# Decoder block on one core: parts of keys and queries stored as they are made, and new orders in the first unit and the handover

## The reference

```python
x_norm = _layernorm(x, norm_g, norm_b)                 # the mamba block, once forward, once on reversed time
xi, z = split(x_norm @ in_w.T);  u = silu(conv(xi) + conv_b)
xdbl = u @ xp_w.T;  dt = softplus(xdbl[..., :16] @ dt_w.T + dt_b);  Bm, Cm = xdbl[..., 16:32], xdbl[..., 32:]
h = exp(dt * A) * h + (dt * u) * Bm;  y = sum(h * Cm)  # a scan over 512 steps, 512 channels x 16 states
y = (y + u * Dp) * silu(z);  x = x + (y_fwd + flip(y_bwd)) @ out_w.T / 2;  x = x + gelu(norm(x) @ w1.T + b1) @ w2.T + b2
scores = q @ k.T / 4, where mask == 0: -1e9            # 16 heads of 16 features, keys and values from the context
out = softmax(scores) @ v @ wo.T + bo
h = relu(norm(x) @ W_fc.T) ** 2;  y = h @ W_proj.T     # then five steps of a threshold unit with reset
```

## Time and profile before

| | |
|---|---|
| time, median of 3 runs | 2777.25 us (2776.8 to 2777.51) |
| profiled execution's own time | 2776.59 us |
| its span (first to last instruction) | 2774.8 us, so 1.8 us lie around it |
| busy in the span | PE 95%, PEld 65%, DVE 79%, ACT 63%, POOL 62% |
| mean granted TensorE clock | 0.98 of full |
| mamba pass, then attention pass | about 1618 us, then 1157 us |

### The profile page before, as it was taken

How to read it: one execution, slowest core, us unless ns; L and a number is a source line. 1 busy time by engine, 2 the same in 40 slices (tenths; PEclk the granted TensorE clock), 3 DMA queues, 4 the chain that set the end, 5 groups by cost and what they waited for, 6 DMA issues and landing times. The chain is left out here.

```text
span 2774.8 us, 55530 instructions
## 1 busy us (share of the span) xinstructions
PE 2633.1 (95%) x19210; PEld 1798.9 (65%) x19210; DVE 2203.8 (79%) x3271; ACT 1743.1 (63%) x2899; POOL 1715.4 (62%) x962
## 2 busy tenths in 40 slices
PE   5999999999999999999999878999999999999996
PEld 2787787787787778877887744455554545454523
DVE  3999999999999899999999959584848484858573
ACT  4778878877877888788778423535354544444342
POOL 1898989988988998899899812323233232323130
PEclk9999999999999999999999989999999999999978
DMA  3122121302221221222122052304040404040300
GB/s 122 33 80 81 63 65 65 103 28 78 88 67 54 79 81 48 79 66 95 36 77 101 9 158 78 99 25 116 8 121 2 121 2 121 2 121 2 106 2 15
DMA packets 102089, 187.07 MB, mean 67 GB/s; under 512 B 14720, under 2 KB 75264, under 8 KB 100256
## 3 DMA queue, kind: packets, MB, share of 16 engines
q1 hardware_dynamic: 101840, 183.92, 21.3%
HBM read 148.38 MB, written 35.52 MB: 66 GB/s over the span
## 5 line engine op out<-in xcount | busy, mean ns | idle before, releaser
L1087 POOL TENSOR_TENSOR hC<-h,C_rep 128x1024 f32<-128x1024 f32 x512 | 1201.3, 2367 | 100.6 <-DVE h L945 94.1
L945 DVE TENSOR_TENSOR_SCAN h<-dA,pair 128x512 f32<-128x512 f32 x1024 | 1171.3, 1201 | 107.8 <-PE pair L467 96.5
L698 ACT ACTIVATE dA<-delta,cols 128x511 f32<-128x511 f32 x1024 | 664.1, 711 | 41.7 <-DVE h L945 28.3
L467 PE MATMUL pair<-diagB,duT 64*128 64x128 f32 x8192 | 549.0, 281 | 23.4 <-DVE h L945 15.2
L467 PEld LDWEIGHTS pair<-diagB,duT 64*128 64x128 f32 x8192 | 486.2, 188 | 124.5 <-issue 92.7
L558 PE MATMUL y_bank<-ident,hC 128*128 128x128 f32 x4112 | 537.3, 277 | 5.5 <-POOL hC L1087 4.5
L558 PEld LDWEIGHTS y_bank<-ident,hC 128*128 128x128 f32 x4112 | 456.3, 141 | 97.7 <-issue 55.7
L1820 DVE CUSTOM_DVE_ANT_0 masked<-pair,mask_bias 128x512 f32<-128x512 f32 x512 | 322.2, 686 | 19.1 <-PE pair L1325 13.5
L1563 ACT ACTIVATE pr<-pair 128x1024 f32<-128x1024 f32 x256 | 248.3, 1021 | 74.3 <-PE pair L1325 74.3
L1922 POOL CAST m_part<-m_rest 8x512 bf16<-8x512 f32 x16 | 9.6, 602 | 429.1 <-ACT m_rest L1563 429.1
L467 PE MATMUL general<-xnT,w_in 128*128 128x512 f32 x512 | 250.5, 605 | 10.9 <-ACT zs L698 5.1
(11 more groups left out here) (177 smaller groups left out, 3166.8 us busy)
## 6 DMA issues: line engine op xcount, KB each, us to landing
C_rep<-c_rows SPq DMA_DIRECT2D x128, 512.0 KB, 4.3
qk_parts<-qk_part SPq DMA_DIRECT2D x96, 256.0 KB, 3.9
w_in<-w_in SPq DMA_DIRECT2D x16, 1024.0 KB, 4.9
k_st<-qk_parts SPq DMA_DIRECT2D x8, 1536.0 KB, 9.1
q_st<-qk_parts SPq DMA_DIRECT2D x8, 1536.0 KB, 9.2
x_in<-x SPq DMA_DIRECT2D x18, 512.0 KB, 5.3
w_out<-w_out SPq DMA_DIRECT2D x17, 512.0 KB, 4.2
mid<-x_out SPq DMA_DIRECT2D x9, 512.0 KB, 4.7
```

Of the source, the lines that this page charges most:

```text
L467: return pe.matmul(o, lhsT, rhs, start=start, stop=stop)
L698: return act.activation(o, i, fn, **kw)
L945: last = dve.tensor_tensor_scan(h[:, g % 4, i, :], dA[:, g % 4, i, :], dBu[:, i, :], 0.0, ALU.mult, ALU.add)
L1087: pool.tensor_tensor(hC[:, g % RING], h[:, g % 4], C_rep[:, 2 * j:2 * j + 2, :], ALU.mult).then_inc(s_hC.sem, 1)
```

## The change

Three places are touched; the arithmetic stays.

1. **Stacks.** The writes of keys and queries to memory go part by part: the three bands of part 0 after `high`, the two of part 1 after `middle`, the one of part 2 after `cut_last`. This holds at the handover and in every iteration.
2. **First unit.** The norms come ahead of `A_log`; z goes to four banks of its own (`first_z`), between the xi blocks; silu of `u` is done by block (`first_u`), `x_proj` follows by block; POOL makes all eight first diagonals, two of them ahead of `make_du`; PE transposes `ab` and spreads the first pair ahead of two of the z blocks of unit 1; ACT makes decays between the z evacuations.
3. **Handover.** The last output projection moves behind `handover` as keys `("lo", jj)`: one half after the key projection, the other after the query projection, which now precede the values. Its add and its store move with it. ACT writes the ones of `k_st`; the row mask work moves behind the query's cuts; sequence 1's `first_norm` no longer waits for the store; POOL's `take_x1(0)` and what follows it wait for the mask tiles, since `mask_i` now lies where `x1` is.

```diff
     (attention_keys)
-    before = many("w2", 2) + many("k", KD) + many("v", 2) + many("qn", KD) + many("q", KD)
+    before = many("w2", 2) + many("k", KD) + [("lo", 0)] + many("qn", KD) + many("q", KD) + [("lo", 1)] + many("v", 2)
     (mamba_pass, PE)
-            for k in range(KI):
+            for k in range(KI - 1):
                 for kk in range(KD):
                     in_proj(("xi", k), 0, 0, k, kk, BEFORE)
-            for k in range(KI):
-                for kk in range(KD):
-                    in_proj(("z", k), 0, 0, k, kk, BEFORE)
+            for k in range(2):
+                first_z(k)
+            for kk in range(KD):
+                in_proj(("xi", KI - 1), 0, 0, KI - 1, kk, BEFORE)
+            for k in range(2, KI):
+                first_z(k)
...
             dt_proj(0, 0, 0, BEFORE)
-            for k in range(KI - 1):
+            for kk in range(KD):
+                in_proj(("xi", KI), 1, 0, 0, kk, BEFORE)
+            for kk in range(KD):
+                in_proj(("z", KI), 1, 0, 0, kk, BEFORE)
+            du_rows(0, 0, 0, BEFORE)
+            pe.wait_ge(kinds["z"][1].sem, kinds["z"][1].count(KI - 1))
+            spread_du(0, 0)
+            for k in range(1, KI - 1):
                 for kk in range(KD):
                     in_proj(("z", KI + k), 1, 0, k, kk, BEFORE)
-            for kk in range(KD):
-                in_proj(("xi", KI), 1, 0, 0, kk, BEFORE)
-            du_rows(0, 0, 0, BEFORE)
-            spread_du(0, 0)
...
-            for jj in range(TT // 2):
-                for half in range(2):
-                    out_proj(jj, half, TT + jj, 2 * B - 1, AFTER)
     (mamba_pass, ACT)
-            act.wait_ge(setup.sem, setup.count(0))
...
+            for k in range(2):
+                first_z(k)
+            first_u(0)
+            start_conv(KI - 1, 0, 0, KI - 1, BEFORE)
+            first_z(2)
+            first_u(1)
+            first_z(3)
+            for k in range(2, KI):
+                first_u(k)
+            act.wait_ge(kinds["z"][1].sem, kinds["z"][1].count(KI - 1))
+            f(zs[0][:, :, :], zs[0][:, :, :], ACT.Silu).then_inc(z_silu.sem, 1)
+            act.preload_act_table_set("natural_log_exp_and_others")
...
-            for j in DIAG_ACT:
-                diagonals(0, j)
-            for k in range(KI - 1):
-                take_z(KI + k, 1, 1, k, BEFORE)
             start_conv(KI, 1, 1, 0, BEFORE)
+            take_z(KI, 1, 1, 0, BEFORE)
             take_du(0, 0, 0, BEFORE)
-            for g in range(3):
-                decay(0, 0, g)
+            act.wait_ge(setup.sem, setup.count(0))
+            decay(0, 0, 0)
+            take_z(KI + 1, 1, 1, 1, BEFORE)
+            decay(0, 0, 1)
+            take_z(KI + 2, 1, 1, 2, BEFORE)
+            decay(0, 0, 2)
     (mamba_pass, POOL)
+            first_diagonals((0, 1))
             make_du(0, 0, 0)
-            for j in DIAG_POOL:
-                diagonals(0, j)
+            first_diagonals(range(2, NP))
     (attention_pass, SP)
-                sp.wait_ge(s_part.sem, s_part.count(2 * beta + n))
-                for band, part in enumerate(which):
-                    dma(s_qkw, qk_dram[n, band].rearrange("(k p) t -> p k t", p=P), qk_part[:, n, part])
+                for part in range(3):
+                    if part < 2:
+                        sp.wait_ge(qk_hi.sem, qk_hi.count(4 * beta + 2 * n + part))
+                    else:
+                        sp.wait_ge(s_part.sem, s_part.count(2 * beta + n))
+                    for band in range(6):
+                        if which[band] == part:
+                            dma(s_qkw, qk_dram[n, band].rearrange("(k p) t -> p k t", p=P), qk_part[:, n, part])
...
-            sp.wait_ge(early.mid.sem, early.mid.count(B))
             x_used(0)
             load_x(1)
...
             stacks(1, 0)
+            sp.wait_ge(kinds["lo"][1].sem, kinds["lo"][1].count(1))
+            dma(early.mid, mid[B * TT:(B + 1) * TT].rearrange("j p f -> p j f"), early.tiles[0][:, :, :])
     (attention_pass, PE)
-            for jj in range(TT // 2):
-                project_v(jj, BEFORE)
+            last_out(0)
+            query_input(0, BEFORE)
             pe.wait_ge(setup_dve.sem, setup_dve.count(0))
...
-            query_input(0, BEFORE)
             project_q(BEFORE)
+            last_out(1)
+            for jj in range(TT // 2):
+                project_v(jj, BEFORE)
     (attention_pass, DVE)
-            dve.memset(k_st[6 * DH:QR, :, :], 1.0)
...
             cut_lo(0, 0)
-            dve.tensor_scalar(keep[:, :, :], maskT_i[:, :, :], 0.0, MASKED, ALU.is_equal, ALU.mult)
+            add_last(0)
...
             cut_last(0, 0)
+            dve.drain()
+            take_q(BEFORE)
+            cut_lo(0, 1)
+            dve.tensor_scalar(keep[:, :, :], maskT_i[:, :, :], 0.0, MASKED, ALU.is_equal, ALU.mult)
+            cut_last(0, 1)
+            add_last(1)
+            first_norm(1)
+            dve.drain()
+            dve.tensor_tensor(mask_biasT[:, :, :], keep[:, :, :],
+                              not_full[:, :].unsqueeze(1).broadcast_to((P, TT, T)), ALU.mult)
             for jj in range(TT // 2):
                 take_v(jj, BEFORE)
...
-            take_q(BEFORE)
-            cut_lo(0, 1)
-            cut_last(0, 1)
-            dve.wait_ge(early.mid.sem, early.mid.count(B))
-            first_norm(1)
     (attention_pass, POOL)
             rstd_of(FF1, 1)
+            pool.wait_ge(setup_dve.sem, setup_dve.count(1))
             take_x1(0)
```

More of the change, by code:

```diff
@@ L71 @@
     gelu: Stage
+@dataclass
+class Late:
+    yT: object
+    w_out: object
+    res: object
 def attention_keys():
@@ L141, in mamba_keys @@
 def mamba_keys():
-    before = [("nf", k) for k in range(KD)] + [("xi", k) for k in range(KI)] + [("z", k) for k in range(KI)]
+    before = [("nf", k) for k in range(KD)] + [("xi", k) for k in range(KI)]
     before += [("xd", 0), ("bt", 0), ("dt", 0)]
-    before += [("z", KI + k) for k in range(KI - 1)] + [("xi", KI), ("tr", 0)]
+    before += [("xi", KI), ("z", KI), ("tr", 0)] + [("z", KI + k) for k in range(1, KI - 1)]
     def batch(units):
@@ L169, in batch @@
         return keys
-    return before, apart(batch(4)), apart(batch(2) + [("yb", 2 * KI)] + [("op", TT + jj) for jj in range(TT // 2)])
+    return before, apart(batch(4)), apart(batch(2) + [("yb", 2 * KI)])
 BEFORE, AFTER = "before", "after"
@@ L500, in x_proj @@
                     pe.wait_ge(s_wxp.sem, s_wxp.count(X))
+                if isinstance(b, str) and b == BEFORE:
+                    pe.wait_ge(first_silu.sem, first_silu.count(kk))
+                elif kk == 0:
                     pe.wait_ge(u_silu.sem, u_silu.count(X))
@@ L815, in _, with first_z, first_u @@
             last.then_inc(a_log.sem, 1)
-            act.wait_ge(setup.sem, setup.count(0))
+            def first_z(k):
+                act.wait_ge(*G.full(("z", k), BEFORE))
+                f(zs[0][:, k, :], bank[k][:, :]).then_inc(G.done_sem(("z", k)), 1)
+            def first_u(k):
+                act.wait_ge(s_tap.sem, s_tap.count((CW - 1) * k + CW - 2))
+                f(u[0][:, k, :], u[0][:, k, :], ACT.Silu).then_inc(first_silu.sem, 1)
             for norm in norm_steps(0):
@@ L988, in add_out @@
                                   ALU.add).then_inc(G.done_sem(("op", i)), 1)
+            first, second = norm_steps(0)
+            for fn in first:
+                fn()
             dve.wait_ge(a_log.sem, a_log.count(0))
@@ L994, in _ @@
             last.then_inc(setup.sem, 1)
-            first, second = norm_steps(0)
-            for fn in first:
-                fn()
             dve.memset(hC[:, :, :, :], 0.0)
@@ L1122, in _, with attention_pass @@
             pool.sem_inc(handover.sem, 1)
-def attention_pass(nc, ctx, a, mid, out, sb, where, stage, psum, consts, handover, early):
+    return Late(yT, w_out, res)
+def attention_pass(nc, ctx, a, mid, out, sb, where, stage, psum, consts, handover, early, late):
     f32, bf16, i32 = mybir.dt.float32, mybir.dt.bfloat16, mybir.dt.int32
@@ L1478, in spike_input, with last_out @@
                 last.then_inc(G.full_sem(key), 1)
+            def last_out(jj):
+                key = ("lo", jj)
+                pe.wait_ge(*G.free(key, BEFORE))
+                bk = G.bank(key, BEFORE)
+                for half_ in range(2):
+                    j = 2 * jj + half_
+                    for k in range(KI):
+                        last = mm(bk[:, half_ * D:(half_ + 1) * D], late.yT[:, k, j * P:(j + 1) * P], late.w_out[:, k, :],
+                                  k == 0, k == KI - 1)
+                last.then_inc(G.full_sem(key), 1)
             pe.wait_ge(early.down.sem, early.down.count(0))
@@ L1766, in spikes, with add_last @@
                 return start, step, finish
-            dve.memset(ones_bf[:, :], 1.0)
+            def add_last(jj):
+                dve.wait_ge(early.mid.sem, early.mid.count(B - 1))
+                dve.wait_ge(*G.full(("lo", jj), BEFORE))
```

(11 more changed lines are left out.)

53 lines of the change are left out of this document (30 added, 23 removed).

## The result

The changed kernel takes 2750.69 us (median of 6 runs, 2748.56 to 2754.75) against 2777.2 for the kernel before beside it (6 runs): a ratio of 0.9907, with an interval of 0.9895 to 0.9919, or 26.5 us less. The forecast was 2751.5. Its profiled execution took 2753.34, with a span of 2751.6, so the two traces differ by only 23.2 us, and what follows is read from that pair first. The forecast sum was 25.8 us. The measured median gain agrees with it, but not by the terms that it was made of.

The account below looks back on a forecast made before the run. PE's own work was taken to bound the loop, leaving gains only in the first unit and handover. Their 15.5 + 10.3 = 25.8 us off the profiled 2776.59 gave 2750.8, with the runs' median 0.66 higher 2751.5; range 2744 to 2761.

Parts of the forecast that it names:

- stacks in the loop: Attention loop: part-by-part writes cost 0 in each of 7 iterations, unless the query read came over 5.5 us later.
- mamba pass behind it: Units after the first: every engine enters the pattern 15.5 us earlier and nothing runs by absolute time, so no change.
- Norms first: First unit, norms ahead of A_log: statistics start earlier, gain 1.5 us (0 to 1.65), passed on to the xi blocks.
- xd: First unit, xi and z interleaved: ACT, last by half a us, is free for xd at 42.7; gain so far 6.2 us.
- From xd to the transposes: First unit: same operations from xd to the end of make_du, 6.7 us; transposes at 49.5 instead of 66.40.
- the first rival: Only one of two gains arrives whole, by slow-rate PE instructions or late masks: 5 to 9 us, 2756 to 2761, chance 0.20.
- POOL's eight diagonals: First unit: 4.7 us more POOL work, six after make_du in 7.1 us, scans and taps at full rate; cost 0 to 1.
- Block start: Handover: output projection, add and store gone, about 1.5 us of block start left; shift 7.5 us (6.5 to 8.3).
- Key parts: Handover: one key write left after the last cut, 3.5 us to the key read instead of 6.4; bounds 2 and 6.4.
- Reads: Handover: products 22.6 us after the key read, first products at 1663.0 instead of 1673.33; splitting the query writes brings nothing.
- The second rival: Handover: query writes do not queue behind the key read; gain 11 to 12 instead of 10.3, 2745 to 2749, chance 0.10.
- Masks: Handover, DVE: 20.3 us from the query's last cut to the first maximum, at 1665.7, almost together with the DMAs.

Follow-up runs that it names:

- experiment 1: The kernel before with only the part-by-part stack writes: ratio 1.0003, 2778.89 us.
- exp. 5: The changed kernel itself, measured again with the same code: ratio 0.9906, 2751.74 us.
- exp. 8: The changed kernel with PE's wait for xd filled by three products that nobody reads: ratio 0.9896, 2749.62 us.
- exp. 3: The kernel before with only the new handover, all six stack writes still after the last cut: ratio 0.9961, 2767.23 us.
- experiment 4: The changed kernel with all six stack writes again after the last cut: ratio 0.9917, 2754.71 us.
- experiment 11: The kernel before with PE's two waits of the first unit filled by unread products (four and five): ratio 0.999, 2774.92 us.
- experiment 9: The kernel before with one wait more, POOL's additions starting only behind the mask tiles: ratio 1.0002, 2778.5 us.
- experiment 12: The changed kernel with DVE's A_log negation behind its memsets and unread products in PE's waits for xd and in the last two mamba units: 0.9902, 2751.0 us.
- experiment 6: The changed kernel with the keys' writes split but the queries' six all behind the last cut: ratio 0.9901, 2751.74 us.

## Why the prediction was right, point by point

| step | forecast | profiled pair | where else |
|---|---|---|---|
| stacks in the loop | 0 | 0 | experiment 1: 0 |
| first unit, gain at the second scan | 15.5 | 12.9 | 13.9 (exp. 5), 15.8 (exp. 8) |
| mamba pass behind it | 0 | -3.3 | -1.9 (exp. 5), -2.5 (exp. 8) |
| handover, gain up to the first products | 10.3 | 13.0 | 9.1 without the split (exp. 3) |
| sum at the first products | 25.8 | 22.6 | 25.1 (exp. 5) |

- **Loop.** Right, with its reason: all six writes and both reads are done long before the products that need them.
- **Norms first.** The statistics started at 4.92, as forecast, but the gain was passed on only where the constants landed in time: second statistics at 12.7 in the profiled execution (12.94 before), at 11.40 in experiment 5. The step treated the landing of the constants as given; ACT could use `eye` 5.5 us after its issue in one execution and 3.8 in the other. The cost of it at xd was 1.4, read against experiment 4, whose first twelve xi products took as long (7.2 us); against experiment 5 it looks like 0.4, because these products took 8.1 there.
- **xd** at 42.58 (forecast 42.7). The order of the steps held, with ACT last as forecast; the tenth is luck. With constants in time, as the forecast assumed, xd came at 41.2 to 42.2, so the interleaving was costed 0.5 to 1.5 too dear, and the late constants hid it.
- **From xd to the transposes** the forecast had 6.8 us and the trace 8.8. This is the step that failed: PE was costed at its full rate behind a wait of 3.1 us, although shows the cold rate behind a wait of 5.12. The forecast had put the end of `x_proj` at 42.2; it was 40.54, and so PE stood idle for long, where the text against the first rival says that its gaps are short. That rival had the price, for other instructions. Experiment 8 gives the size: 2.0 us at the transposes against the profiled execution, 1.2 to 1.9 between xd and S against all six without the filling. Another 0.8 was lost from the transposes to S (9.1 for 8.3), where ACT's second z evacuation ends 7.4 behind the transposes instead of 6.9, and S follows that by 1.7 instead of 1.4. What the page on TensorE's clock in the Trainium skill ("TensorE: Matmul & The Clock Gate", "HAM oscillation — how this bites in real kernels") describes in general, a wait that makes the next burst cold, these rows show for waits of 3.14, 2.79 and, in experiment 11, 2.16 us.
- **POOL's eight diagonals** cost 7.09 us for six and lay beside taps and scans that ran at full rate: one tap 0.75, two scans 2.33 (2.32 before). That was the pair no trace had shown. The Trainium skill, "SBUF — State Buffer", "Who interferes with whom", says that a DVE instruction with at most one SBUF input, outside the two-port modes, does not contend with GpSimd. The trace agrees with these numbers.
- **The mamba pass.** "Nothing runs by absolute time" was true of the code and not of the time. In all nine profiled executions with the new first unit the distance from S to the last gelu is 1537.6 to 1540.3, in all five with the old one 1536.8 to 1537.0. Of this, 0.5 lies between S and the next unit's load of `w_out` (30.43 against 29.93; 30.84 in experiment 9). Another 1.9 is regular: every second unit takes 96.35 us instead of 96.08, seven times over. The rest comes and goes by executions: the last unit but one takes 89.68 or 90.75 with either first unit. The half clock is not the cause of these, by experiment 12. Where the 0.27 arises can be read: at one place in DVE's queue, between the last `delta` of a unit and the next scan, first before, then after:

```profile
191.09 0.66 DVE L936 SCALAR_TENSOR_TENSOR delta<-general,ab 128x512 f32<-128x512 f32 x1
...
192.27 3.44 DVE L945 TENSOR_TENSOR_SCAN h<-dA,pair 128x512 f32<-128x512 f32 x3
```

```profile
178.72 0.67 DVE L972 SCALAR_TENSOR_TENSOR delta<-general,ab 128x512 f32<-128x512 f32 x1
...
180.17 3.44 DVE L981 TENSOR_TENSOR_SCAN h<-dA,pair 128x512 f32<-128x512 f32 x3 [0.19 <-PE pair L475]
```

The scan follows `delta` by 1.45 us instead of 1.18, in all seven such units of all nine executions and in none of the other five. The register instructions that DVE's queue has between the two start 0.3 us behind `delta` instead of 0.02, and the trace shows nothing that they wait for. Why stays open. Experiment 11, meant to test whether the place of the code does it, cannot tell: it adds instructions to PE's program alone and leaves DVE's as it was (its units took 96.07 to 96.15), while the new first unit reorders DVE's program ahead of the loop.
- **Block start** behind the last gelu: 1.25 including the gelu's end, so 0.56 and not 1.5. The gain was 8.4 (forecast 7.5, upper bound 8.3).
- **Key parts.** Cut to read 2.2 (forecast 3.5). The step scaled the issue time of six writes; but what stays is one write's issue and landing, and the five others had landed meanwhile.
- **Reads.** 22.2 from key read to products (forecast 22.6), with early query writes, late ones (experiment 6), or none split (22.3 in experiment 4). The prediction took its 22.6 from "both places of the trace"; only the handover shows it, since in the loop the products wait for PE's other work and follow the key read by 28.15. The rule quoted from the Trainium skill, "DMA: Bandwidth & Descriptors", stood the test that it offered. The second rival is out.
- **Masks.** 18.9 us from the queries' last cut to the first maximum (forecast 20.3). With the products at 1650.74 DVE was 2.9 us late, which experiment 9 shows to be free. So here the prediction was wrong in its picture and right in its number: the masks are no second bound at some 3 us late, they are one at the 7.28 us of experiment 1 (no run lies between the two), and the handover's whole gain counts. POOL's `take_x1` ran beside the first maxima, whose pitch stayed 0.61: no cost, as forecast.
- **A gain that was not in the sum.** The new block start waits 1.3 us instead of 2.8, and the down projection behind it was never cold. Two of five executions before paid 3.05 for it, so it is worth about 1.2 on average (an estimate from five). The medians differ by 26.5 where the profiled pair differs by 23.2: the profiled execution after was 2.65 above its median, and the one before, with a warm down projection, 0.6 under its own.

So the agreement of the sum is in part luck. In the profiled pair the first unit gained 2.6 less than forecast and the mamba pass gave back 3.3, against a handover that was 2.7 better: 3.2 short in all, and 0.7 short in experiment 5. The median of 2750.69 fits the forecast of 2751.5 because errors of both signs partly cancel, and because, by the estimate above, some 1.2 us came from a cold down projection that no term of the sum held; the rest is within what the executions scatter by (2748.56 to 2754.75). The version with the wait filled (experiment 8) has the lowest median of all, 2749.62; its interval does not part it from the changed kernel.

## What to carry to other kernels

Cost PE's instructions behind a wait of some 3 us at the half-clock rate of a row, and if a wait can't be removed, fill it with products that nobody reads and look at the granted clock. Before an edit is given a price, find the engine that comes last at that place: splitting the writes was worth 0 where DVE came 7 us behind the products, and 3.9 in the trace once it did not. A shift of a long regular stretch is not passed on whole: compare the length of its repeated pieces, not only its ends, and find the first instruction in a piece that comes late.

## What the runs showed of the hardware that I had not expected

- The granted clock fell behind a wait of 2.16 us in experiment 11 (0.50 from 52 to 54 us). Behind a wait of 2.79 us 64 products took 17.1 us in two of five executions and 14.05 in three. Behind a wait of 1.3 us they took 14.05 in nine of nine.
- The half clock lasts differently in executions of the same code: in the windows 44 to 50 us of the first unit it was 0.50, 0.50, 0.60 in the one and 0.50, 0.83, 1.00 in the other (experiment 5), and from xd to the second scan they took 17.89 and 17.26 us.
- The time from the key read's issue to the query stack's use was 22.2 to 22.8 us in all fourteen profiled executions, while the first query writes were issued 1.5 to 6.3 us behind that read: the latest writes (6.3, experiment 6) went with 22.3 us, the earliest (1.5, experiment 12) with 22.5.
- One waiting instruction on POOL made a DVE normalisation four times as fast (5.51 to 1.38 us) and the kernel no faster at all.
- A reordering of DVE's program ahead of a loop came with 0.27 us between two DVE instructions deep in that loop, at the same place in 63 of 63 units (1.45 instead of 1.18 us), with no wait on record for it.
